# Two scan schedules and one normalising operand: a two-layer image network on one NeuronCore

## The reference

```python
# x: (1, 256, 256, 128). _gn: group norm with 32 groups of 4 channels, no affine.
x = x + attention(_gn(x))      # layer 0
x = x + scans(_gn(x))          # layer 1

def attention(z):              # 4 heads of 32, over the 256 tokens of each row
    zn = layernorm(z) * ln_scale + ln_bias
    q, k, v = zn @ Wq, zn @ Wk, zn @ Wv
    bias, g = zn @ Wb, sigmoid(zn @ Wg)
    a = softmax(q k^T / sqrt(32) + bias)
    return (g * (a v)) @ Wo

def scans(x):                  # D_INNER 256, D_STATE 16, DT_RANK 8, K = 4 directions
    xi, z = split(x @ w_in.T); z = silu(z)
    xc = silu(depthwise_conv3x3(xi) + conv_b)
    # the directions: rows, columns, and both reversed; 65536 tokens each
    dts, Bs, Cs = split(x_proj_w[k] @ xs[k])
    delta = softplus(dt_w[k] @ dts + dt_b[k])
    # for each token, 256 channels x 16 states:
    h = exp(delta * A) * h + (delta * x) * B
    y = sum_n h[n] * C[n] + D * x
    y = sum of the four directions, each put back in its order
    return (layernorm(y) * ln_w + ln_b) * z @ w_out.T
```

## Time and profile before

| | |
|---|---|
| median of 3 runs | 24477.81 us (24476.09 to 24478.5) |
| profiled execution | 24484.89 us |
| its span, first to last instruction | 24483.1 us, mean granted TensorE clock 0.989 |
| PE, PE weight loads | 23673.9 us (97%), 21232.5 us (87%) |
| DVE | 23428.3 us (96%) |
| ACT | 22643.4 us (92%) |
| POOL | 20836.7 us (85%) |
| four scans | first scan at 3442.9 us, last at 23796.2 us |
| normalising | first product at 146.7 us, last at 544.8 us |

### The profile page before, as it was taken

One profiled execution on the slowest core, in us unless ns is written; L12 is line 12 of the kernel. 1 busy time (PEld: TensorE's weight loads), 2 busy tenths in 40 slices (PEclk: granted clock), 3 DMA queues, 4 the chain that ended last, 5 costly groups with the idle time before them and its releaser, 6 DMA issues. The chain is left out here.

```text
span 24483.1 us, 521206 instructions
## 1 busy us (share of the span) xinstructions
PE 23673.9 (97%) x197836; PEld 21232.5 (87%) x197836; DVE 23428.3 (96%) x23356; ACT 22643.4 (92%) x45591; POOL 20836.7 (85%) x6924
## 2 busy tenths in 40 slices
PE   4997989999999999999999999999999999999999
PEld 1776469999999999999999899999999999999987
DVE  6999889999999999999999999999999999999996
ACT  3997569999999999999999999999999999999986
POOL 5000039999999999999999999999999999999997
PEclk8998999999999999999999999999999999999999
DMA  5222555555555555555555566666666666666665
GB/s 185 58 58 94 176 183 184 187 182 188 184 187 186 179 188 189 189 187 190 189 187 190 187 195 195 194 197 193 197 196 190 194 197 192 198 193 195 196 198 189
DMA packets 3815251, 4429.66 MB, mean 181 GB/s; under 512 B 2085380, under 2 KB 3140520, under 8 KB 3532584
## 3 DMA queue, kind: packets, MB, share of 16 engines
q1 hardware_dynamic: 3812776, 4396.31, 55.4%
HBM read 3782.68 MB, written 617.09 MB: 180 GB/s over the span
## 5 line engine op out<-in xcount | busy, mean ns | idle before, releaser
L1470 DVE TENSOR_TENSOR_SCAN s_h<-s_da,s_h,s_db 128x512 f32<-128x512 f32 x16256 | 19208.5, 1260 | 251.2 <-PE s_db L1371 250.5
L1488 POOL TENSOR_TENSOR s_prod<-s_h,s_cb 128x2048 f32<-128x2048 f32 x4096 | 18617.4, 4574 | 448.8 <-DVE s_h L1470 440.9
L1440 ACT ACTIVATE s_da<-s_delta,a_neg 128x512 f32<-128x512 f32 x16384 | 10895.5, 716 | 181.8 <-DVE s_h L1470 149.2
L1384 PE MATMUL s_py<-eye,s_prod 128*128 128x128 f32 x65536 | 8505.7, 273 | 18.2 <-POOL s_prod L1488 17.6
L1429 ACT ACTIVATE s_dxb<-s_dx,s_btok 128x256 f32<-128x256 f32 x18944 | 8411.7, 502 | 32.1 <-PEq L63 32.1
L1371 PE MATMUL s_db<-s_bdiag,s_dx 128*128 128x128 f32 x51200 | 8399.5, 275 | 0.0
L1384 PEld LDWEIGHTS s_py<-eye,s_prod 128*128 128x128 f32 x65536 | 7416.1, 141 | 27.6 <-POOL s_prod L1488 22.4
L1367 PE MATMUL s_db<-eye,s_dxb 128*128 128x128 f32 x39936 | 7178.5, 276 | 156.2 <-ACT s_dxb L1429 116.9
L1371 PEld LDWEIGHTS s_db<-s_bdiag,s_dx 128*128 128x128 f32 x51200 | 7012.3, 192 | 0.0
L1367 PEld LDWEIGHTS s_db<-eye,s_dxb 128*128 128x128 f32 x39936 | 4806.9, 141 | 1156.4 <-issue 626.4
L542 POOL COPY a_spread<-a_rden 128x256 f32<-128x256 f32 x256 | 103.1, 403 | 1646.0 <-DVE a_rden L504 1646.0
(11 more groups left out here) (139 smaller groups left out, 16397.8 us busy)
## 6 DMA issues: line engine op xcount, KB each, us to landing
s_cb<-c_rows SPq DMA_DIRECT2D x2048, 1024.0 KB, 5.5
s_bdiag<-b_diag SPq DMA_DIRECT2D x2048, 256.0 KB, 5.1
s_bdiag<-b_diag SPq DMA_DIRECT2D x1536, 192.0 KB, 6.7
y<-s_yt SPq DMA_DIRECT2D x1024, 256.0 KB, 2.7
s_xc<-xc_own SPq DMA_DIRECT2D x384, 512.0 KB, 9.3
s_yb<-y SPq DMA_DIRECT2D x768, 256.0 KB, 4.2
xc_tok<-c_ot SPq DMA_DIRECT2D x32, 2048.0 KB, 7.6
s_xt<-xc_tok SPq DMA_DIRECT2D x256, 256.0 KB, 5.3
```

Of the source, the lines that this page charges most:

```text
L1384: last = e.matmul(out, prod[:, i // TOGETHER % GROUPS_KEPT, i % TOGETHER, half, j * P:(j + 1) * P], const["eye"][:, :], start=first, stop= ...
L1440: last = e.activation(da[:, i % NDA, half, :], delta[:, g % 2, half, :], ACT.Exp, scale=wts[k]["a_neg"][:, half, n:n + 1])
L1470: last = e.tensor_tensor_scan(h[:, n, half, flow], da[:, i % NDA, half, flow], db[:, i % NDB, half, flow], first, ALU.mult, ALU.add)
L1488: e.tensor_tensor(prod[:, p % GROUPS_KEPT], h[:, states], columns.unsqueeze(2).to_broadcast([P, TOGETHER, HALVES, T]), ALU.mult).then_inc( ...
```

## The change

`norm_phase`: a PSUM tile of one bank gets the scale and the shift written out to 128 channels each, once, by VectorE; the two products of each chunk read them there, broadcast over the 16 blocks. `scans_phase`: where the pieces of `ADDED` and the skip term stand in directions 2 and 3; state 6 has one diagonal instead of two in directions 0, 2 and 3; and the tables for directions 0, 2 and 3 put dts, exp, log and delta one step later (in direction 0 turnb and btok too).

```diff
--- before.py
+++ after.py
@@ -159,12 +159,12 @@
         bt = m.sb("n_bt", [HEADS, 2, CT])
         tp = m.ps("n_tp", [P, 4, BANK])
         bp = m.ps("n_bp", [P, 2, BANK])
+        rows = m.ps("n_rows", [P, BANK])
         src = x.rearrange("(q b p) c -> q p b c", b=BLOCKS, p=P)
         bdst = bias_d.rearrange("h (q t) -> q h t", t=CT)
-        four = lambda v: v.rearrange("p b (g c) -> p b g c", c=PER_GROUP)
-        row = lambda v: v[:, :].unsqueeze(1).unsqueeze(3).to_broadcast([P, BLOCKS, GROUPS, PER_GROUP])
+        row = lambda i: rows[:, i * C:(i + 1) * C].unsqueeze(1).to_broadcast([P, BLOCKS, C])
         S = signals(sems, "load0 load1 load2 store0 store1 bstore0 bstore1 "
-                          "scaled shifted stats aggr var rstd nmr std normed turned evac pair bevac")
+                          "rows scaled shifted stats aggr var rstd nmr std normed turned evac pair bevac")
         halves = (slice(0, BLOCKS // 2), slice(BLOCKS // 2, BLOCKS))
         with nc.Block() as block:
             @block.sync
@@ -208,9 +208,9 @@
                     e.wait_ge(S[f"load{l}"], 2 * DMA * (q // LOADS + 1))
                     if q >= AFFINE:
                         e.wait_ge(S["turned"], 4 * (q - AFFINE) + 4)
-                    e.tensor_tensor(four(gt[:, g]), four(xt[:, l]), row(scale_row), ALU.mult).then_inc(S["scaled"], 1)
+                    e.tensor_tensor(gt[:, g], xt[:, l], row(0), ALU.mult).then_inc(S["scaled"], 1)
                     e.wait_ge(S["scaled"], q + 1)
-                    e.tensor_tensor(four(gt[:, g]), four(gt[:, g]), row(shift_row), ALU.add).then_inc(S["shifted"], 1)
+                    e.tensor_tensor(gt[:, g], gt[:, g], row(1), ALU.add).then_inc(S["shifted"], 1)
                     e.wait_ge(S["shifted"], q + 1)
                     for j in range(BLOCKS):
                         last = e.bn_stats(st[:, s, j, :], gt[:, g, j, :])
@@ -232,6 +232,10 @@
                     e.scalar_tensor_tensor(out=nmr[:, s], in0=mv[:, s, :, 0], scalar=-1.0, in1=rstd[:, s],
                                            op0=ALU.mult, op1=ALU.mult).then_inc(S["nmr"], 1)
 
+                for i, of in enumerate((scale_row, shift_row)):
+                    e.tensor_copy(rows[:, i * C:(i + 1) * C].rearrange("p (g c) -> p g c", c=PER_GROUP),
+                                  of[:, :].unsqueeze(2).to_broadcast([P, GROUPS, PER_GROUP])).then_inc(S["rows"], 1)
+                e.wait_ge(S["rows"], 2)
                 begin(0)
                 for q in range(N):
                     if q + 1 < N:
@@ -865,7 +869,8 @@
     SUBS_ACT = 3
     STEPS = TILES * D_STATE
     SKIP = {2: 0, 3: 1}
-    ADDED = {1: (5, 9), 2: (6, 13), 3: (6, 13)}
+    ADDED = {1: (5, 9), 2: (8, 11), 3: (8, 11)}
+    SKIPPED = 2
     SHARE = 2
     CSLOTS = 3
     backwards = lambda k: k >= 2
@@ -873,7 +878,7 @@
     turned_in = lambda k: k == 1
     shared = lambda k: k == 1
     on_pool = lambda k, n, j: shared(k) and n % SHARE == SHARE - 1 and j == SUBS_ACT - 1
-    second_diagonal = lambda k, n: not shared(k) and n % GROUP != 0
+    second_diagonal = lambda k, n: not shared(k) and n % GROUP != 0 and n != 6
     scaled_subs = lambda k, n: SUBS_ACT - 1 if second_diagonal(k, n) else SUBS_ACT
     diagonals = lambda k: 1 if shared(k) else 2
     c_rows, dt_rows, b_rows, b_tokens = kept_rows
@@ -1100,9 +1105,9 @@
                 e.tensor_tensor(e1(s), delta[:, s], xc[:, s], ALU.mult).then_inc(S["doubled"], 1)
 
         PLAN_KEPT = {
-            "PE": {-2: "proj0", 0: "proj1", 2: "turnb", 4: "dts", 11: "turnd"},
-            "ACT": {1: "low", 5: "exp", 6: "log", 12: "dx"},
-            "DVE": {3: "btok", 7: "delta"},
+            "PE": {-2: "proj0", 0: "proj1", 3: "turnb", 5: "dts", 11: "turnd"},
+            "ACT": {1: "low", 6: "exp", 7: "log", 12: "dx"},
+            "DVE": {4: "btok", 8: "delta"},
             "POOL": {4: "double"},
         }
         PLAN_KEPT_FIRST = {
@@ -1124,9 +1129,9 @@
             "POOL": {},
         }
         PLAN_BACK = {
-            "PE": {1: "dts", 9: "turnd"},
-            "ACT": {2: "exp", 3: "log", 10: "dx"},
-            "DVE": {4: "delta"},
+            "PE": {2: "dts", 9: "turnd"},
+            "ACT": {3: "exp", 4: "log", 10: "dx"},
+            "DVE": {5: "delta"},
             "POOL": {3: "double"},
         }
         START = Tile(d=0, t=0, s=0, n=1, own=1, turns=0, lines=0, lows=0, doubled=1)
@@ -1395,7 +1400,7 @@
                                                 start=False, stop=False, skip_group_check=True)
                                 if bank == 1:
                                     last.then_inc(S["added"], 1)
-                        if n == GROUP and k in SKIP:
+                        if n == SKIPPED and k in SKIP:
                             half = SKIP[k]
                             for j in range(SUBS):
                                 out = py[:, j // 2, (j % 2) * D_INNER + half * P:(j % 2) * D_INNER + (half + 1) * P]
```

## The result

| | before | after |
|---|---|---|
| median | 24477.9 us | 24351.4 us (24350.2 to 24351.8, 4 runs) |
| ratio to before | | 0.9948 [0.9935, 0.996] |
| span of the profiled execution | 24483.1 us | 24349.2 us |
| normalising, first product to last | 398.1 us | 312.3 us |
| tile of direction 0 (127 distances) | 39.32 us | 38.86 us |

The change saves 126 us; the forecast was 267, and the time lies 1.4 us above the range. By parts, up to the first scan it gave -89 (3354.1 us instead of 3442.9; 86 of them between the first and the last product of normalising), direction 0 -0.46 x 127 = -58, and the backward directions +0.054 x 254 = **+14**, where -137 was forecast. The sum, -133, agrees with the difference of the spans, -134.

A forecast was written before the change was run, and what follows sets the result against it. Backward tiles were taken as bound by TensorE's own work, over VectorE's, plus stalls from bunched pieces. Directions 2 and 3 -137, direction 0 -42, normalising -88 sum to -267 us: 24211 us, range 24130 to 24350.

The forecast's parts named there:

- TensorE's ledger: Backward tile: TensorE's work, priced from starts, sums to 39.0 us, over VectorE's 38.6; 38.8 with state 6 single.
- The old gaps before scans 3 and 12: VectorE's two waits for TensorE's s_db in each direction 2 tile, one 0.64 us, the other smaller; both forecast to go.
- What is late next ... I follow the ring once round: Backward tile: copies, log, delta, scans 6 to 8, turn of state 10, next copies; sum 39.11 us, taken as 39.15.
- the whole backward term: Directions 2 and 3: -0.54 us a tile x 127 x 2 = -137 us, bounds -215 and -50.
- State 6 with one diagonal: Directions 0, 2, 3: TensorE -0.23 us a tile, ScalarE +0.40, covered by idle time of 0.9 (direction 0) and 1.4 (direction 2).
- Rival 2: Backward tile gains nothing, stall moves from s_db to a 1 us delta wait: 24348 us; chance 0.15.
- the prediction's own signs of being wrong: Delta's gap over 1 us, TensorE's wait for s_db persisting, or GpSimd's normalising mean staying near 684 ns.
- Rivals 1 and 5: Backward tile falls to TensorE's 38.84, 24132 us, chance 0.12; or TensorE has room, VectorE's 38.61, 24074 us, chance 0.03.
- Rival 4: ScalarE misses a step, delta waits 2.03 us beyond the forecast: 24727 us; decides from 1.6 us; chance 0.07.
- Direction 0: Stall before scan 6 goes nearly whole; tile 38.99 us, -0.33 x 127 = -42 us, bounds -60 and -10.
- Normalising: PSUM rows free GpSimd; a chunk takes 10.0 us instead of 12.84, -88 us, bounds -102 and 0.
- Rival 3: GpSimd is not freed in normalising: 24299 us; chance 0.10.

The follow-up runs named there:

- The kernel in which TensorE is all that is left: Changed kernel with backward log at step 5, delta at 6, and state 14 instead of 6 on one diagonal in directions 2 and 3: 24114.2 us, ratio 0.9851.
- The dead piece behind the log: Changed kernel plus an unread third ScalarE scaling piece in directions 2 and 3: for state 7 24453.4 us, for state 14 24353.8 us.
- the rows in SBUF: Changed kernel with normalising's written-out scale and shift rows in SBUF instead of PSUM: 24433.8 us, ratio 0.9982.
- the old table: Changed kernel with the earlier backward table (dt step 1, exp 2, log 3, delta 4): 24431.0 us; with delta at 5: 24146.2 us.

## Why the prediction was wrong, step by step

- **TensorE's ledger**: right. The kernel in which TensorE is all that is left shows 38.80. The prices that the prediction prints sum to 38.96, so to 38.73 with state 6 single and 38.79 with its 0.06 for the switch after dt; its 38.84 is not quite what they give. The old gaps before scans 3 and 12 went, as forecast.
- **"What is late next ... I follow the ring once round"**: this step failed, and with it the whole backward term. The place was right (the log behind the copies), and so was the kind of stall, the delta waiting 0.57 for ScalarE. But the ring was closed over the delta, scans 6 to 8 and the turn of state 10 (39.11). ScalarE is in order: behind the log stands the scaling for state 7, and TensorE's turn of 7 wants it before anything that comes from the delta. From the rows of before that ring would have summed to 0.94 + 1.21 + 1.22 + 0.95 for the log + 0.81 + 0.05 = 5.18 on ScalarE, and on TensorE to the forecast's own 26.40 and, ahead of it, step 6 with the skip term 3.10, step 7 1.98, step 8 2.20 and the first half of the turn of 10, 0.66, = 34.34: 39.52, 0.4 more than the ring that was taken, against 39.74 measured. The dead piece behind the log, 0.40 at state 7 and nothing at 14, shows which ring binds.
- **State 6 with one diagonal**, booked as -0.23 on TensorE with 1.4 us of ScalarE idle time as its cover: the cover was an average. In the backward ring the piece costs 0.40 and the relief, which lies in the turn of 6 outside the ring, gives nothing. ScalarE's idle time is now 1.27 us a tile, 0.63 before the copies and 0.54 before the exp, which waits for dts. Both stand before the piece, where ScalarE waits for TensorE, so they are no room for work that comes behind the copies.
- **Rival 2**, that the backward tile gains nothing and the stall moves to the delta: this is what happened (24348 against 24351), but its delta wait of 1 us was 0.57, and the rest of the stall is at `s_db`, 0.34 before scan 4. That the `s_db` wait persists was one of the prediction's own signs of being wrong. The rival had no mechanism, its price came from assuming no gain, and that it met the total within 3 us is luck in part: direction 0 gave 16 us more than the forecast had for it, and the backward tiles lost 14 us where the rival had nothing.
- **Rivals 1 and 5**: log later with the single at 14 arrives at 38.80, so rival 1's 38.84 was the right size for a schedule without the ring. 38.61 was reached by none of the runs. **Rival 4** needed a delta wait of 1.6 us; in the runs it was 0.57 at most in nearly all tiles.
- **Direction 0**: right in its way, and the gain was underrated by 0.13 a tile (38.86 for 38.99). The walk that left the turn of 7 a margin of 0.02 was good; the forecast left 0.04 of stall and 0.1 for the log, and neither is there: VectorE's tile has no gap left. The log ends 0.03 before VectorE gets to it.
- **Normalising**: right, 10.07 us a chunk for 10.0, -86 for -88, GpSimd 220.9 us for 225. **Rival 3** (not freed) is what the rows in SBUF make: 335.6 us and 24434. The plain broadcast by itself gives nothing.

This case's runs bear out what the Trainium skill, "SBUF — State Buffer", section "SBUF: two separate sides", says of the port pair that VectorE and GpSimd share, that a VectorE operation with two SBUF inputs takes it whole against a GpSimd operation that reads SBUF: 335.6 us with both operands in SBUF, 220.9 with one in PSUM. The 62 cycles more for a PSUM source, which the Trainium skill, "VectorE: DVE Perf Modes", section "The TRN2 errata", gives and the prediction weighed, are not seen: the product with the PSUM operand takes 2281 ns in the median (2278 to 2289), the one with SBUF alone took 2348 and at least 2283, and 2284 at least with the rows in SBUF. The prediction's own comparison could not tell, since two lengths, one with each kind of operand, fit any fixed part.

## What to carry to other kernels

When an in-order engine gets an instruction moved to a new place, look first at what stands directly behind it in that queue and who wants that; close the ring over the earliest such consumer, and sum every ring that passes through the move, not one. In these runs an instruction cost its full length inside the ring that set the period and nothing outside it, until another ring became the longest, whatever the idle share of its engine said, so work that is to buy another engine relief is put at a step outside all rings. Where VectorE reads two SBUF operands beside a GpSimd that works in SBUF, one operand in PSUM can give GpSimd its time back (335.6 us to 220.9 here).

## What was not expected of the hardware

- Two dead pieces of the same form, 0.40 us each, gave 102 us and 2 us, by their step alone.
- Deferring the delta by one step in the old table took 24431 to 24146: an instruction that runs earlier than it is needed held up VectorE's states, then GpSimd's products, then TensorE's totals, three engines away.
- TensorE is full at 949 us of weight loads in 1000 (38.80 us a tile, all of it accounted for by starts).
